# Expert weights of a two-stage mixture-of-experts kernel: experts 4 to 15 loaded at other places in the ScalarE program

## What is computed

```python
shared = _silu_and_mul(x @ shared_gate_up_w.T) @ shared_down_w.T          # width 704
shared = shared * sigmoid(x @ sgate_w.T)
routing_weights = softmax(x @ gate_w.T)                                   # 16 experts
topk_w, topk_ids = top_k(routing_weights, 4)
def body(acc, (w13_e, w2_e, e)):                                          # each expert, width 176
    coef = sum(where(topk_ids == e, topk_w, 0.0), axis=-1)
    h = _silu_and_mul(x @ w13_e.T)
    return acc + (h @ w2_e.T) * coef[:, None]
x = x + shared + sparse_out            # x is layer-normed on the way in
```

## Time and profile before

| what | us |
|---|---|
| median of 3 runs | 1238.4 (1236.88 to 1241.4) |
| the profiled execution, whole | 1242.44 |
| its span, from first to last instruction | 1240.6 |
| first expert stage: scatters begin, last lands, last expert tile turned | 365.4, 420.5, 535.3 |
| second expert stage, the same | 1052.5, 1106.8, 1219.5 |

### The profile page before, as it was taken

The page is one execution under the profiler, slowest core; times in us unless marked ns, Lnnn a source line. Parts: engine busy times, 40 slices in busy tenths (PEclk is TensorE's granted clock), DMA queues, the critical chain, the costliest instruction groups (busy, mean ns, idle before and its releaser), DMA issues.

```text
span 1240.6 us, 23045 instructions
## 1 busy us (share of the span) xinstructions
PE 1167.9 (94%) x7483; PEld 1004.9 (81%) x7484; DVE 806.6 (65%) x2038; ACT 752.8 (61%) x1734; POOL 602.5 (49%) x497
## 2 busy tenths in 40 slices
PE   6999999999898799989999999999999999879997
PEld 5888888888776577667999999999999997657775
DVE  6767767776874333377777777777777778433335
ACT  5866667666642233336888888878887875323332
POOL 3111222112126465624777667777777742646663
PEclk9999999999998899999999999999999998989999
DMA  3366666763257477651422222222222114836666
GB/s 115 86 175 176 180 163 168 184 171 69 64 175 246 122 137 134 121 118 43 99 60 75 61 59 59 64 63 62 70 79 59 34 48 138 265 129 121 111 116 146
DMA packets 94897, 141.59 MB, mean 114 GB/s; under 512 B 8292, under 2 KB 74084, under 8 KB 94180
## 3 DMA queue, kind: packets, MB, share of 16 engines
q1 hardware_dynamic: 74400, 102.32, 30.8%
q0 software_dynamic: 15744, 20.98, 10.1%
q10 hardware_dynamic: 4676, 17.30, 4.6%
HBM read 99.71 MB, written 40.86 MB: 113 GB/s over the span
## 4 chain that ended last, share of the span: by engine, by line
PE 73%; DMA 10%; DVE 5%; POOL 5%; issue 4%; ACT 2%; SPq 0%; DVEq 0%; ACTq 0%; POOLq 0%
PE ps L276 18%; PE ps L278 18%; PE ps L277 18%; PE ps L1116 6%; DMA sums_d<-e_y,xg 4%; PE ps L1141 4%; POOL slots_d L1288 4%; DMA slots_d<-rows,slot_i 2%; DMA rows_a<-a_rows_d 2%; PE ps L551 2%; PE ps L1129 1%; PE ps L1093 1%; PE ps L1683 1%; PE ps L565 1%; DMA xg<-slots_d 1%
## 5 line engine op out<-in xcount | busy, mean ns | idle before, releaser
L1294 POOL DMA_INDIRECT sums_d<-e_y,xg x88 | 137.7, 1565 | 102.8 <-ACT e_y L1219 63.3
L1415 DVE COPY e_hT<-ps 88x256 f32<-88x256 f32 x94 | 39.5, 420 | 153.5 <-PE ps L1129 144.7
L1116 PE MATMUL ps<-w,e_xT 128*128 (+1 forms) x376 | 130.0, 469 | 2.4 <-issue 1.1
L427 POOL TENSOR_TENSOR aw_lo<-aw_raw,aw_hi 128x512 fp32r<-128x512 f32 x32 | 41.8, 1309 | 153.2 <-ACT aw_hi L423 153.2
L276 PE MATMUL ps<-xn_hi,aw_hi 128*128 128x512 f32 x256 | 111.2, 435 | 2.0 <-DVE bmat_lo L790 1.8
L857 DVE TENSOR_TENSOR m_a<-ps,e_a 128x384 f32<-128x384 f32 x128 | 71.2, 556 | 58.0 <-PE ps L551 57.5
L278 PE MATMUL ps<-xn_hi,aw_lo 128*128 128x512 f32 x256 | 101.4, 396 | 0.0
L277 PE MATMUL ps<-xn_lo,aw_hi 128*128 128x512 f32 x256 | 100.9, 394 | 0.0
L1141 PE MATMUL ps<-w,e_hT 88*128 (+1 forms) x376 | 97.7, 382 | 0.0
L1288 POOL DMA_INDIRECT slots_d<-rows,slot_i x64 | 65.7, 1027 | 64.4 <-DVE slot_i L1480 23.8
L656 ACT COPY late<-ps 128x256 f32<-128x256 f32 x128 | 47.8, 373 | 69.5 <-PE ps L278 69.4
(11 more groups left out here) (311 smaller groups left out, 4133.0 us busy)
## 6 DMA issues: line engine op xcount, KB each, us to landing
rows_a<-a_rows_d SPq DMA_DIRECT2D x64, 256.0 KB, 5.0
xg<-slots_d SPq DMA_DIRECT2D x94, 144.0 KB
slots_d<-slot_init SPq DMA_DIRECT2D x10, 1152.0 KB, 6.8
wconv_raw<-b_conv SPq DMA_DIRECT2D x16, 513.0 KB, 3.5
aw_raw<-a_heads SPq DMA_DIRECT2D x32, 256.0 KB, 3.1
wvo_raw<-b_vo SPq DMA_DIRECT2D x16, 512.0 KB
rows_b<-b_rows_d SPq DMA_DIRECT2D x32, 256.0 KB, 4.9
w<-moe_up ACTq DMA_DIRECT2D x4, 1408.0 KB
```

What stands on the lines that cost most here:

```text
L427: return nc.gpsimd.tensor_tensor(dst[1], src, f32(dst[0]), ALU.subtract).then_inc(sem(done_sem), 1)
L1116: ins = nc.tensor.matmul(ps[:, 2 + t % 2, 0:2 * E_HIDDEN], e_xT[:, t % 2, k], weights_of(w13, t, at_w, k * 2 * E_HIDDEN, 2 * E_HIDDEN), st ...
L1294: nc.gpsimd.indirect_dma_start(sums_d[f][t % CHAINS], bass.IndirectOffsetOnAxis(ap=xg[:, t % XG, ROW_ID:ROW_ID + 1].bitcast(U32), axis=0), ...
L1415: nc.vector.tensor_copy(e_hT[0:HALF_E, t % 2], ps[0:HALF_E, 4 + t % 2, 0:2 * P].rearrange("p (j m) -> p j m", j=2)).then_inc(sem("e_hT"), 1)
```

## The change

Experts 0 to 3 stay. Experts 4 to 7 become two pairs: 4 and 5 right after the two Exp, 6 and 7 behind shared tile 1. Experts 8 to 15 leave the shared part and are issued as pairs in the expert loop, in its passes 0, 2, 4 and 6, between the copy of the turned tile `t + 1` and the SiLU of tile `t`. The wait counts of TensorE follow. Bytes, waits of TensorE by tile and all else are the same.

```diff
-        W_LOADS = [GROUP_E // n for n in (GROUP_E, GROUP_E, 2, 2)]
+        W_LOADS = [GROUP_E // n for n in (GROUP_E, 2, 2, 2)]
+        W_TILES = {0: 8, 2: 10, 4: 12, 6: 14}
...
-            for g in range(2):
-                f_weights(act, g * GROUP_E, GROUP_E)
+            f_weights(act, 0, GROUP_E)
             routed(act, "dve", f, "shift")
             nc.scalar.activation(pr[:], pr[:], ACT.Exp).then_inc(sem("f_route_act"), 1)
             nc.scalar.activation(sg[:], sg[:], ACT.Exp).then_inc(sem("f_route_act"), 1)
+            f_weights(act, GROUP_E, 2)
             f_silu_act(act, f, 0, 1)
...
-                if 2 * GROUP_E + 2 * (i - 1) < EXPERTS:
-                    f_weights(act, 2 * GROUP_E + 2 * (i - 1), 2)
+                if i == 1:
+                    f_weights(act, GROUP_E + 2, 2)
             routed(act, "dve", f, "w_at")
             for t in range(-1, TILES + 2):
                 if t + 1 < TILES:
                     e_xT_act(act, f, t + 1)
+                if t in W_TILES:
+                    f_weights(act, W_TILES[t], 2)
                 if 0 <= t < TILES:
                     e_silu_act(act, f, t)
```

## The result

The changed kernel takes 1246.12 us in the median of 16 runs (1241.28 to 1249.15); the kernel before, run beside it, 1239.82 (1236.16 to 1243.16, 16 runs). The ratio is 1.0049, 95% interval 1.0037 to 1.0060: **6.1 us slower**, where the forecast had it 1.4 us faster. The time lies inside the overall range given (1229 to 1247) and outside the forecast's own (1232 to 1243), and the direction is wrong. The profiled execution of the changed kernel has a span of 1245.7 us against 1240.6.

A forecast was written before the change was run, and what follows sets the result against it. The bound was taken as GpSimd's scatter rounds in the shared part and TensorE's 2.49 us a tile in the expert part. Gain -10.4 plus cost 9.0 gave -1.4 us, median 1238.4 to 1237.0; own range 1232 to 1243, overall 1229 to 1247.

The forecast's parts named there:

- Pass 2: Expert loop: its pair is triggered at the copy of tile 3, before the first add exists, so free of the adds.
- the gain: Shared part, scatter rounds: 5.6 us in the first stage and 4.8 in the second, 10.4 together, bounds 5 and 14.
- if all later rounds ran as the quiet one: Shared part: three later scatter rounds at 11.57 us each, gaining 6.8 and 6.3 us in the two stages before deductions.
- I kept 0.7 and 0.4 us of its excess: First scatter landing, 1.94 and 1.47 us over the quiet one: 0.7 and 0.4 counted as gain, with pair 6, 7 on it.
- the row used for pass 0: Scatter started at 403.36, just before a weight trigger: 5.58 us instead of 2.43, the upper bound for the last round.
- 9.14 + 0.3: Scatter round two: issuing eight scatters at the quiet 9.14 us, plus 0.3 for raw tile 5.
- Pass 0: Its pair, 8 and 9, falls on the last scatters of the shared part: 1.4 us taken, between nothing and 3.15.
- The adds: Expert part: pairs of passes 4 and 6 each delay the add chain 3.15 us, less 2.4 slack; 4.5 a stage, 9.0 together.
- Fair queues: Rival, expert part: adds and tile loads get turns under a pair, cost 1.6 us, sum -8.8, 1229.6 us; chance 0.26.
- Starved adds: Rival: pairs of passes 4 and 6 run together and hold an add; cost 15.6, gain 6.9, +8.7, 1247.1 us; chance 0.18.
- no gain in the shared part: Rival: scatters hold one another up, not the weights; some 4 us gained, 4 lost, 1238 us; chance 0.05.
- Slower: Whole kernel: chance 0.20 of a slower result, beside faster 0.27 and same 0.53, where same means within 6.2 us.

The follow-up runs named there:

- e1_gain_alone: The changed kernel without the four expert-loop loads, experts 8 to 15 using the weights of 0 to 7; ratio 0.9945 to the kernel before, -6.8 us.
- e11_pass0_only: e1_gain_alone with one load in the loop, experts 8 and 9 in pass 0; ratio 0.9955 to the kernel before.
- e1_repeat: e1_gain_alone once more, the floor without any load in the expert loop; ratio 0.9931 to the kernel before, -8.5 us.
- e2_cost_alone: The kernel before, with experts 12 to 15 loaded a second time over themselves in passes 4 and 6; ratio 1.0085, +10.5 us.
- e6_tile2: e3_pass1 with experts 6 and 7 issued behind shared tile 2 instead of tile 1; ratio 0.9979 to the kernel before.
- e0_again: The changed kernel once more, no edit, for a second profile; ratio 1.0046 to the kernel before, +5.7 us.
- e10: e8 with experts 12 and 13 loaded one at a time in passes 6 and 9 instead of behind shared tile 3; ratio 0.9991 to the kernel before.
- e8: e3_pass1 with experts 6, 7 behind shared tile 2, 12, 13 behind 3, 14, 15 behind 4, and 8 to 11 in passes 1, 2; ratio 0.9949, -6.3 us.
- e3_pass1: The changed kernel with its pair of pass 0 moved to pass 1; ratio 1.0023 to the kernel before, +2.8 us.
- e7: e3_pass1 with experts 12 to 15 issued as pairs behind shared tiles 2 and 3, only 8 to 11 in the loop; ratio 0.9966, -4.2 us.

## Why the prediction was wrong

**The sum, term by term.** The three experiments that take one part alone add up to the whole, within their intervals:

| term | forecast, us | measured, us | by |
|---|---|---|---|
| shared part without any load in the loop | -13.2 | -7.7 | e1_gain_alone and its repetition |
| pair of pass 0 on a scatter round | +2.8 | +3.0 | e11_pass0_only against e1_repeat |
| pairs of passes 4 and 6 beside the adds | +9.0 | +10.5 | e2_cost_alone |
| sum | -1.4 | +5.8 | the change: +6.1 and +5.7 |

(The forecast's -10.4 held the pass 0 term of 1.4 a stage.) Pass 2 was costed at nothing, and nothing is left for it in the sum; but the intervals of the three terms, taken together, leave some 4 us to either side, and no kernel had pass 2 alone.

**The step that failed is the gain**, by 5.5 us: "if all later rounds ran as the quiet one", less small deductions. In the profile of e1_gain_alone the shortfall sits in three places. (1) The first landing: I kept 0.7 and 0.4 us of its excess, by which it would have been 3.7 and 3.5 us; it was 4.49 and 4.58, no better than in the kernel before. The pair behind tile 1 was triggered at 370.8 in the changed kernel, as I had worked out; I underpriced what it does there, though the row used for pass 0 (3.15 us more) stood beside it; e6_tile2 showed its whole price by taking it away: 2.48. (2) The second landing of the first stage: 4.84 where I took 2.43. That I could not have read from the rows shown: what delays it is the instruction packet, which in the kernel before came at 399.6, in the middle of round three, where no landing was near. (3) Round two took 9.9 and 9.8 us to issue and not 9.14 + 0.3, though the last weights were through before it; so the traffic to which I had put the 10.02 us of before was not what made it slow. What did stays open. The third and fourth rounds ran as forecast. Only e0_again, the execution in which the packet missed the landing, had nearly the forecast's gain (5.5 and 4.6 us to the turn of tile 3).

**Pass 0** was wrong in place, and that its size came out is luck. It was put at 1.4 us on the last landing of both stages; it hits the third, costs about 2.7 us in the first stage and nothing in the second, and not in every execution. TensorE's end came 9 us earlier (turn of tile 0 at 402.4 instead of 411.6), not the six I took.

**The adds** were right in road and near in price: an add of 4.61 + 3.15 = 7.76 us was the step, 7.73 stands in the first profile, and adds 1 and 2 under a first pair took 6.0 to 9.6 in all the kernels with pairs in pass 4. What I left out is that the tile load behind the add meets the second pair as well (4.6 to 7.1 us, and 8.7 for one that met the first pair itself, where I took 2.1). That may be why e2_cost_alone has 10.5 and not 9.0; the difference lies inside its interval of 2.3 us to either side.

**Fair queues.** Here were read for more than they show. Between 378 and 380 only the last packets of the scatter of 374.66 were due (the next one was issued at 379.29), while between 1102 and 1104 scatters followed each other; 4 packets against 96 don't compare like with like. The changed kernel's trace has the better case: add 1 was issued at 428.80, and its packets, which come 2.2 us after the issue for the undisturbed add 0, were due at 431.0. The list of queues between 431 and 433, while the up weights of a pair end and its down weights begin, and then between 433 and 434, in the last quarter of its bytes:

```profile
q10 hardware_dynamic: 162, 0.62, 88.8%
q0 software_dynamic: 6, 0.01, 11.3%
...
q10 hardware_dynamic: 91, 0.18, 68.4%
q0 software_dynamic: 40, 0.04, 24.4%
```

In the first window, where ScalarE's packets are 3.8 KB in the mean (0.62 MB in 162), the add gets 6 packets; in the second, at 2 KB, it moves. The Trainium skill's page "DMA: Bandwidth & Descriptors", section "Queues, rings and completion order", says that each engine takes its queues by turns, a packet from each; the trace agrees with that in the second window and not in the first. Why, the runs don't show: the up and down weights differ in packet size, in rows and in coming first, none of these was varied alone, and the add's packets may also have been handed over late.

**The chances.** Of the rivals none was it whole. "Starved adds" had the right direction, from 12 us of cost on; the cost was 10.5, and the sum went positive because the gain was smaller. That case, the gain at its own lower bound (5) with the cost of 9.0, lay inside the bounds and would have given +4. The rival "no gain in the shared part" came nearest to it, but it was priced with 4 us of cost where the sum had 9.0, had another mechanism (scatters that hold one another up, which the 2.4 us landings of round three in e1_gain_alone and e3_pass1 rule out) and a chance of 0.05. Slower had 0.20 in all, where this case alone deserved as much.

What stays open: why the two singles of e10 cost 5 us against e8. Their profiles differ by 4.4 us: e10 takes 3.9 more for turns 4 to 46 (107.4 and 106.7) and 2.3 less up to tile 3 (50.6 in both stages against 52.6 and 50.9), and 2.1 us of the difference lie ahead of the first scatter, where the two programs are the same. So part of the 5 us may be no effect of the edit.

## What to carry to other kernels

In this kernel a bulk load did not cost its bytes; it cost what waited on a small transfer's landing while it drained. Where small DMAs follow each other freely, as within a scatter round, 1 MB beside them was free (in e3_pass1 eight scatters took 9.1 us, as in quiet, with the pair triggered among them at 407.3); where each waits for an earlier one, as the adds do, the same 1 MB cost its delay once the slack was gone, and the delay was not won back by tile 46. So put bulk loads at the start of a stretch that only issues, keep them away from its last transfer, and before counting the gain of removing one cause of a late landing, price each other load that still lies on it.

## What the runs showed of the hardware

A 16 KB packet of instructions took one of the 16 DMA engines for 0.93 us in the changed kernel (up to 1.65 in the others), and a scatter landed only with the last of its 16 closing packets: fifteen by 391.0, the sixteenth at 391.97, the landing at 393.06. A scatter of 2.43 us then took 4.08 to 4.84. The packet of the second stage came 20.5 us after the first scatter in both profiles of the changed kernel; before the change it was 27.0. So it moves with the program, and a stage that is changed can run into it.

Under a pair of 1056 KB on ScalarE's queue, an accumulating add (1 or 2) took 6.0 to 9.6 us instead of 3.7 to 4.6, a scatter up to 6.65 (the second landing of e7, which may hold an instruction packet too) instead of 2.43, a tile load of 144 KB 4.6 to 8.7 instead of 2.1.
